# Projections: the short filter of the values on ScalarE and VectorE, sums of squares by GpSimd and small products

## The chip, the cores and the metric

The kernel runs on one of the eight cores of a Trainium2 chip. A core has TensorE (matrix products; the trace gives the clock that was granted to it, as a share of full speed), VectorE, ScalarE and GpSimd (elementwise work, each in its own program order), and a SyncE queue that issues most transfers. In the profile they are PE, DVE, ACT, POOL and SP. Operands lie in SBUF, results of TensorE in PSUM. The metric is the device time of the whole program in microseconds (us). Timelines give the start of an instruction in us from the start of the span.

## The reference

One transformer layer of batch 4, 2048 tokens, width 256, 4 heads of 64: a modulated layer norm, an attention of the delta-rule kind with two causal filters on the values (3 and 31 taps), a router that mixes the branches, an output projection, and a mixture of 16 small experts with a shared one. What matters here are the projections, their four-tap causal filters, and what the later stages take from them (sketched in few lines):

```python
q = silu(causal_dwconv(x @ Wq, conv_q))      # 4 taps per channel
k = silu(causal_dwconv(x @ Wk, conv_k))
v = silu(causal_dwconv(x @ Wv, conv_v))
q = q * rsqrt(sum(q * q, per head) + 1e-6)   # the same for k
fs = fir(v, fir_short)                       # 3 taps per channel
```

The kernel does not scale q and k in this stage. It stores them as they are, and keeps the eight factors per token, `(sum + 1e-6) ** -0.5`, in `rn`, which stays in SBUF.

## The kernel before

The program is a row of stages, each a block that ends when all engines have finished (`EARLY`, `LATE`, `LAST` in `build`): setup, norm_inputs, conv_heads, long_filter, chunk_inverses, delta_scan, mix_and_experts. The change is in conv_heads (L418) and in setup. Tokens come in 16 units of 512 (`NU`, `UT`), a unit in four tiles of 128 (`J`).

A unit has six blocks of 128 channels (`NBLK`), two of k, two of q, two of v. For a block, TensorE multiplies (`project`, into two PSUM buffers `cv_pj`), with the channels on the partitions and the tokens in the free dimension. ScalarE copies the product to `cv_pre` and, scaled by the filter's last tap, to `cv_acc` (`evacuate`, L568). VectorE adds the three other taps, one scalar_tensor_tensor each over 512 tokens, each of which waits for the one before (`conv`, L652). ScalarE applies silu (`silu`, L597) into `cv_kqc` or `cv_vT`; after the sixth block it copies the last columns of `cv_pre` and `cv_vT` to the next unit's buffers (`halo`, `vhalo`).

Later stages want tokens on the partitions. TensorE therefore turns the tiles of k and q (`turn_kq`, into `cv_kqps`) and of v (`turn_v`, into `cv_vfps`). The three-tap filter of the values is made in the second: three products of shifted columns with diagonal matrices `diag_fs` that setup has written. A product of 32-bit operands is two passes in the trace, a transpose is one. ScalarE copies k out (`cv_k`), squares k and q (`cv_sq`), and copies values and filtered values out (`cv_vf`). VectorE sums the squares per head (`reduce_sq`), GpSimd adds the epsilon (L682) and takes the power -1/2 (L686). q is turned for its squares alone: it is stored untouched from `cv_kqc`.

Nothing plans this order; it is written out. `units_ahead` (L240) runs `front(0)` and then `body(u)` for each unit. A body has six slots. In slot s each engine does its share of block s of unit u+1 (`project`, `front_slot`, `conv`) and, in fixed places around it, a tile of unit u's turning. Each engine is strictly in order, so a wait holds up all that is behind it. VectorE's `conv` of block 0 waits for ScalarE's `evacuate` of block 0; ScalarE's `evacuate` of block 0 stands behind `silu`, `halo` and `vhalo` of the unit before, since those are in that unit's slot 5.

## Time and profile before

| | |
|---|---|
| three runs | 2955.58, 2953.98, 2932.95 us (median 2953.98) |
| profiled execution: its time, its span | 2923.57 us, 2921.5 us |
| TensorE's granted clock, mean | 0.896 |
| busy over the span: TensorE, VectorE, ScalarE, GpSimd | 89%, 57%, 38%, 21% |
| conv_heads within the span | first product at 189.5 us, last copy ends at 506.4, next stage's first transfer at 511.7 |
| 288 filter steps of VectorE | 215.7 us busy, 750 ns each |

The busy time of an engine is the time in which an instruction of it is in flight, also where that instruction waits inside the engine. Start to start, two instructions behind one another can be closer than the first one's length. The timeline names for an instruction how long its engine idled before it and what ended that idling. A name that begins with `cv_` belongs to this stage, with `mx_` to the last one.

### The profile page before, as it was taken

What the parts mean: (1) busy time and instruction counts of PE and PEld (TensorE: products, weight loads), DVE (VectorE), ACT (ScalarE), POOL (GpSimd) and SP (SyncE); (2) the same over time, 40 slices, a digit from 0 to 9 for tenths busy, and PEclk for the clock granted to TensorE, in tenths of its full rate; (3) what the DMA queues carried; (4) which work ended last, traced back from release to release, by engine and by line L of the source; (5) the groups of instructions that cost most, each with busy time, mean ns of one, the idle gap of its engine ahead of it and who ended that gap; (6) DMA issues with size and microseconds to landing.
All of it is one profiled execution on the core that took longest, in us unless ns stands there. A gap on an engine that the chain in (4) does not pass through costs nothing.

```text
span 2921.5 us, 40764 instructions
## 1 busy us (share of the span) xinstructions
PE 2613.2 (89%) x14016; PEld 1883.8 (64%) x14016; DVE 1657.9 (57%) x4330; ACT 1108.4 (38%) x2270; POOL 610.6 (21%) x417
## 2 busy tenths in 40 slices
PE   4989998344899799966999999999999999999998
PEld 3966666333688688854666666666656666666665
DVE  3438886220990355535565755675566557665765
ACT  1237787324766222221333233323333333233321
POOL 1105555003110111112122212221222122121210
PEclk7569999675679899986999999999999999999999
DMA  3425555976877677621011101110110111011000
GB/s 92 144 80 173 164 157 162 233 169 139 190 180 187 204 230 240 196 80 44 1 51 51 51 1 52 51 42 10 51 52 16 36 51 51 1 51 51 8 1 15
DMA packets 349603, 274.04 MB, mean 94 GB/s; under 512 B 166413, under 2 KB 306125, under 8 KB 347877
## 3 DMA queue, kind: packets, MB, share of 16 engines
q1 hardware_dynamic: 337680, 256.90, 30.4%
q0 software_dynamic: 3456, 12.58, 1.6%
q10 hardware_dynamic: 8276, 2.10, 0.4%
q8 instruction: 110, 1.80, 0.3%
q14 instruction: 81, 0.66, 0.1%
HBM read 170.65 MB, written 100.89 MB: 93 GB/s over the span
## 4 chain that ended last, share of the span: by engine, by line
PE 37%; DVE 8%; POOL 8%; issue 3%; DMA 0%; POOLq 0%; ACT 0%; DVEq 0%; SPq 0%; ACTq 0%
PE mx_dn L1807 12%; PE mx_up L1793 11%; POOL mx_st L1693 4%; PE mx_m L1746 4%; DVE mx_acc L2098 3%; PE mx_m L1747 2%; PE mx_m L1755 2%; PE mx_m L1770 2%; POOL mx_rms L1704 2%; DVE mx_t L1960 1%; PE mx_m L1784 1%; POOL mx_acc L1711 1%; PE mx_m L1756 1%; POOL mx_acc L1714 1%; DVE mx_t L1962 1%
## 5 line engine op out<-in xcount | busy, mean ns | idle before, releaser
L2098 DVE SCALAR_TENSOR_TENSOR mx_acc<-mx_dn,mx_comb,mx_acc 128x256 f32<-128x256 f32 x1024 | 424.4, 477 | 483.1 <-PE mx_dn L1807 481.0
L1807 PE MATMUL mx_dn<-mx_edn,mx_hs 128*128 128x256 f32 x2048 | 513.2, 396 | 3.3 <-ACT mx_hs L1876 3.3
L1807 PEld LDWEIGHTS mx_dn<-mx_edn,mx_hs 128*128 128x128 f32 x2048 | 398.6, 198 | 168.1 <-issue 95.3
L1793 PE MATMUL mx_up<-mx_h2T,mx_eup 128*128 128x512 f32 x1024 | 500.3, 612 | 0.0
L1876 ACT ACTIVATE mx_hs<-mx_up 128x512 f32<-128x512 f32 x320 | 190.0, 596 | 799.1 <-PE mx_up L1793 798.8
L1793 PEld LDWEIGHTS mx_up<-mx_h2T,mx_eup 128*128 128x128 f32 x1024 | 190.6, 193 | 157.6 <-issue 148.6
L652 DVE SCALAR_TENSOR_TENSOR cv_acc<-cv_pre,conv_w,cv_acc 128x512 f32<-128x512 f32 x288 | 215.7, 750 | 86.9 <-ACT cv_acc L574 80.1
L516 PE MATMUL cv_pj<-cv_hT,wqkv 128*128 128x512 f32 x384 | 181.3, 602 | 14.0 <-ACT cv_acc L574 8.0
L1698 POOL TENSOR_TENSOR mx_t<-mx_vf,mx_ids 128x1024 f32<-128x1024 f32 x16 | 31.5, 1966 | 650.4 <-DVE mx_pr L1955 650.4
L1087 PE MATMUL ci_gps<-ci_kT 64*128 64x128 f32 x768 | 96.9, 412 | 55.4 <-DMA ci_kT<-kqT_d 48.3
L1693 POOL TENSOR_TENSOR mx_st<-mx_tmp,root_pow 128x24 f32<-128x24 f32 x32 | 132.9, 4168 | 31.1 <-DVE mx_tmp L1926 31.1
L806 PE MATMUL fl_ps<-fl_toep,fl_vc 128*84 128x98 f32 x512 | 56.1, 277 | 91.5 <-DMA fl_toep<-taps_d 45.6
L686 POOL TENSOR_TENSOR rn<-cv_ss,half_pow 128x8 f32 x64 | 129.0, 2015 | 11.7 <-POOL cv_ss L682 11.7
L1155 ACT ACTIVATE ci_A<-ci_gps,ck 128x128 f32<-128x128 f32 x384 | 106.0, 373 | 61.2 <-PE ci_gps L1087 61.2
L1807 PEld LDWEIGHTS mx_dn<-mx_sdn,mx_hs 128*128 128x128 f32 x512 | 97.4, 190 | 40.4 <-issue 30.6
L1087 PEld LDWEIGHTS ci_gps<-ci_kT 64*128 64x128 f32 x768 | 79.0, 287 | 68.7 <-DMA ci_kT<-kqT_d 52.0
L1746 PE MATMUL mx_m<-mx_hT,wr 128*128 128x512 f32 x256 | 122.6, 602 | 0.8 <-ACT mx_stT L1836 0.8
L1793 PE MATMUL mx_up<-mx_h2T,mx_sup 128*128 128x512 f32 x256 | 120.0, 602 | 1.4 <-issue 1.4
L1807 PE MATMUL mx_dn<-mx_sdn,mx_hs 128*128 128x256 f32 x512 | 121.0, 379 | 0.0
L516 PEld LDWEIGHTS cv_pj<-cv_hT,wqkv 128*128 128x128 f32 x384 | 67.5, 192 | 74.2 <-issue 54.0
L1488 ACT ACTIVATE ds_U<-ds_ups 64x256 f32<-64x256 f32 x64 | 24.1, 377 | 239.1 <-PE ds_ups L1381 239.1
L806 PEld LDWEIGHTS fl_ps<-fl_toep,fl_vc 128*84 128x84 f32 x512 | 53.5, 178 | 94.1 <-DMA fl_toep<-taps_d 47.2
(229 smaller groups left out, 4399.1 us busy)
## 6 DMA issues: line engine op xcount, KB each, us to landing
kqT_d<-cv_kqc SPq DMA_DIRECT2D x16, 1024.0 KB, 8.0
vf_d<-cv_vf SPq DMA_DIRECT2D x16, 1024.0 KB, 5.3
ds_kqT<-kqT_d SPq DMA_DIRECT2D x16, 1024.0 KB, 5.7
mx_vf<-vf_d SPq DMA_DIRECT2D x16, 1024.0 KB, 6.3
fl_toep<-taps_d SPq DMA_DIRECT2D x32, 392.0 KB, 5.4
ci_kT<-kqT_d POOLq DMA_DIRECT2D x24, 512.0 KB, 5.9
fl_pool<-vf_d SPq DMA_DIRECT2D x8, 1216.0 KB
xin<-_attn_hidden_states_dram SPq DMA_DIRECT2D x16, 512.0 KB, 3.9
```

Of the source, the lines that this page charges most:

```text
L516: ins = pe.matmul(pj[o % 2][:], m.wqkv[:, k, weight(o) * P:(weight(o) + 1) * P], hT[i][:, k, :], start=(k == 0), stop=(k == KD - 1))
L652: ins = dve.scalar_tensor_tensor(out=acc[o % 3][:], in0=pre[i][:, o, t:t + UT], scalar=m.conv_w[:, weight(o), t:t + 1], in1=acc[o % 3][:], ...
L686: pool.tensor_tensor(m.rn[:, bass.ds(u * (J * 2 * H) + j * 2 * H, 2 * H)], ss[j % 2][:], m.half_pow[:, 0:2 * H], ALU.pow).then_inc(rn_done, 1)
L806: ins = pe.matmul(ps[r][0:NA, c // 4, (c % 4) * WIN:(c % 4 + 1) * WIN], vc[:, ch, :], toep[q][:, n * CB + c, ::-1], start=True, stop=True)
L1087: ins = pe.matmul(g_ps[n % 2][h % 2][:, h // 2 * P:(h // 2 + 1) * P], kT[k % 2][r, b, h // 2, :], kT[k % 2][r, b, h // 2, :], start=True, ...
L1155: ins = act.activation(a[:, b, h, :], g_ps[n % 2][h % 2][:, h // 2 * P:(h // 2 + 1) * P], ACT.Identity, scale=m.ck[:, c + h:c + h + 1])
L1693: pool.tensor_tensor(std[:, :, 1, :], tmp[:, 2, part].rearrange("p (a h) -> p a h", h=H), m.root_pow[:, part].rearrange("p (a h) -> p a h" ...
L1746: pe.matmul(out[:], m.wr1[:, k, f * P:(f + 1) * P], hT[i][:, k, :], start=(k == 0), stop=False)
L1793: ins = pe.matmul(up_ps[x % 2][:], lhs, h2T[i][:, k, :], start=(k == 0), stop=(k == KD - 1))
L1807: ins = pe.matmul(dn_ps[(i + n) % 2][:, j, :], hs[x % 4][:, j * P:(j + 1) * P], rhs, start=(x == 0 and j % 2 == 0) or x >= NS, stop=(x >= ...
L1876: act.activation(hs[x % 4][:], up_ps[x % 2][:], ACT.Silu).then_inc(silu_done, 1)
L2098: ins = dve.scalar_tensor_tensor(out=acc[i][:, j, :], in0=dn_ps[(i + n) % 2][:, j, :], scalar=comb[i][:, j, e:e + 1], in1=acc[i][:, j, :], ...
```

## The change

In setup the six diagonal matrices are gone; the filter's weights `fs_w` stay in SBUF as they are loaded.

In conv_heads:
- The value filter is computed with channels on the partitions. ScalarE multiplies `cv_vT` by the last tap into a new tile `cv_ff` (`last_tap`); VectorE adds the two other taps with one scalar_tensor_tensor of 512 tokens each (`fir`), placed between the steps of `conv` in slots 0 and 1. `turn_v` turns both `cv_vT` and `cv_ff` with transposes alone, and moves from slots 1 to 4 to slots 3, 4 and, for two tiles, 5; its evacuation on ScalarE moves with it (`put_vf`).
- Only k is turned (`turn_k`), two tiles into one PSUM bank, with one copy of 512 columns per bank.
- GpSimd squares the four blocks of k and q from `cv_kqc`, and TensorE sums them per head: per tile and block a product with a 128x2 matrix of ones and zeros (`pick`), eight columns a tile, into `cv_ssps`. VectorE adds the epsilon for all four tiles at once, GpSimd takes one power of 32 columns.

The diff, without the declarations of tiles and semaphores:

```diff
--- before.py
+++ after.py
...
@@ -220,12 +219,6 @@
                         .then_inc(vec_step, 1)
             n = 8 + B * KD
 
-            for k in range(KD):
-                for t in range(FIRS):
-                    dve.tensor_scalar(m.diag_fs[:, k, t, :], m.ident[:], fs_w[:, k, t:t + 1], None, ALU.mult)\
-                        .then_inc(vec_step, 1)
-            n += KD * FIRS
-
             dve.wait_ge(act_step, 4)
             for h in range(H):
                 dve.scalar_tensor_tensor(out=m.rtau[:, h:h + 1], in0=taus[:, 4 + h:5 + h], scalar=0.0,
...
@@ -485,7 +485,7 @@
                 sp.wait_ge(silu_done, u * NBLK + (NKQ + 3))
                 sp.dma_start(m.kqT_d[rows].rearrange("j p (a c) -> p a j c", a=NKQ),
                              kqc[i][:].rearrange("p a (j c) -> p a j c", j=J)).then_inc(kqT_store[i], 16)
-                sp.wait_ge(k_done, u * J + (J + 2))
+                sp.wait_ge(k_done, u * 2 + 4)
                 sp.dma_start(m.k_d[rows].rearrange("j p c -> p j c"), k[i][:]).then_inc(store[i], 16)
                 sp.wait_ge(vfe_done, u * J + (J + 2))
                 sp.dma_start(m.vf_d[rows].rearrange("j p c -> p j c"), vf[i][:]).then_inc(store[i], 16)
...
@@ -505,6 +505,7 @@
         @block.tensor
         def _(pe):
             pe.sem_inc(pre_done, 2)
+            pe.wait_ge(pick_done, 3)
 
             def project(u, g, o):
                 i = g % 2
...
@@ -520,28 +521,38 @@
             def turn_v(u, g, j):
                 i = g % 2
                 if j == 0:
-                    pe.wait_ge(silu_done, u * NBLK + (NBLK + 3))
-                    pe.wait_ge(vhalo_done, u + 1)
+                    pe.wait_ge(fir_done, u * KD + KD)
                 pe.wait_ge(vfe_done, u * J + (j + 1))
                 c0 = j * P
                 for k in range(KD):
                     pe.transpose(vf_ps[j % 2][:, k * P:(k + 1) * P],
                                  vT[i][:, k, FIRS - 1 + c0:FIRS - 1 + c0 + P], m.ident[:])
                 for k in range(KD):
-                    for t in range(FIRS):
-                        ins = pe.matmul(vf_ps[j % 2][:, D + k * P:D + (k + 1) * P], vT[i][:, k, c0 + t:c0 + t + P],
-                                        m.diag_fs[:, k, t, :], start=(t == 0), stop=(t == FIRS - 1))
+                    ins = pe.transpose(vf_ps[j % 2][:, D + k * P:D + (k + 1) * P], ff[i][:, k, c0:c0 + P], m.ident[:])
                 ins.then_inc(vf_done, 1)
 
-            def turn_kq(u, g, j):
+            def turn_k(u, g, y):
+                if y == 0:
+                    pe.wait_ge(silu_done, u * NBLK + (NKQ + 3))
+
+                pe.wait_ge(k_done, u * 2 + (y + 1))
+                for j in two:
+                    c0 = (2 * y + j) * P
+                    for k in range(KD):
+                        ins = pe.transpose(k_ps[y][:, j * D + k * P:j * D + (k + 1) * P],
+                                           kqc[g % 2][:, k, c0:c0 + P], m.ident[:])
+                ins.then_inc(kt_done, 1)
+
+            def sum_sq(u, g, j):
+                i = g % 2
                 if j == 0:
-                    pe.wait_ge(silu_done, u * NBLK + (NKQ + 3))
-
-                pe.wait_ge(sq_done, u * J + (j + 1))
-                for a in range(2 * KD):
-                    ins = pe.transpose(kq_ps[j % 2][:, a * P:(a + 1) * P], kqc[g % 2][:, a, j * P:(j + 1) * P],
-                                       m.ident[:])
-                ins.then_inc(kq_done, 1)
+                    pe.wait_ge(sq_done, u * NKQ + NKQ)
+                    pe.wait_ge(eps_done, u + 1)
+                for a in range(NKQ):
+                    ins = pe.matmul(ss_ps[i][:, j * 2 * H + a * 2:j * 2 * H + a * 2 + 2], sq[i][:, a, j * P:(j + 1) * P],
+                                    pick[:], start=True, stop=True)
+                if j == J - 1:
+                    ins.then_inc(ss_done, 1)
 
             def front(u, g):
                 for o in range(NBLK):
...
@@ -551,10 +562,17 @@
                 for s in range(NBLK):
                     if nxt is not None:
                         project(nxt, g + 1, s)
-                    if s < J:
-                        turn_kq(u, g, s)
-                    if 1 <= s < J + 1:
-                        turn_v(u, g, s - 1)
+                    if s < 2:
+                        turn_k(u, g, s)
+                    if s == 1:
+                        sum_sq(u, g, 0)
+                    if s == 2:
+                        for j in range(1, J):
+                            sum_sq(u, g, j)
+                    if s >= 3:
+                        turn_v(u, g, s - 3)
+                    if s == NBLK - 1:
+                        turn_v(u, g, J - 1)
 
             units_ahead(pe, front, body)
 
...
@@ -586,7 +604,7 @@
             def vhalo(u, g):
 
                 if not isinstance(u, int) or u > 0:
-                    act.wait_ge(vf_done, u * J)
+                    act.wait_ge(fir_done, u * KD)
                 if g % UB == UB - 1:
                     src = m.zeros[:, 0:KD * (FIRS - 1)].rearrange("p (a b) -> p a b", a=KD)
                 else:
...
@@ -598,9 +616,16 @@
                 i = g % 2
                 if o == 0:
                     act.wait_ge(kqT_store[i], (u - i) * 8 + 16)
+                    act.wait_ge(ss_done, u + 1)
                 act.wait_ge(conv_done, u * NBLK + (o + 1))
                 dst = kqc[i][:, o, :] if o < NKQ else vT[i][:, o - NKQ, FIRS - 1:]
                 act.activation(dst, acc[o % 3][:], ACT.Silu).then_inc(silu_done, 1)
+
+            def last_tap(u, g, k):
+                i = g % 2
+                act.wait_ge(silu_done, u * NBLK + (NKQ + k + 4))
+                act.activation(ff[i][:, k, :], vT[i][:, k, FIRS - 1:], ACT.Copy, scale=m.fs_w[:, k, FIRS - 1:FIRS])\
+                    .then_inc(tap_done, 1)
 
             def front_slot(u, g, s):
                 evacuate(u, g, s)
...
@@ -610,38 +635,43 @@
                     silu(u, g, s)
                     halo(u, g)
                     vhalo(u, g)
+                    for k in range(KD):
+                        last_tap(u, g, k)
 
             def front(u, g):
                 for s in range(NBLK):
                     front_slot(u, g, s)
 
+            def put_vf(u, i, j):
+                act.wait_ge(vf_done, u * J + (j + 1))
+                act.activation(vf[i][:, j, :], vf_ps[j % 2][:], ACT.Copy).then_inc(vfe_done, 1)
+
             def body(u, g, nxt):
                 i = g % 2
 
                 act.wait_ge(store[i], (u - i) * 16 + 32)
                 for s in range(NBLK):
-                    if s < J:
-                        act.wait_ge(kq_done, u * J + (s + 1))
-                        act.wait_ge(red_done, u * J + (s + 1))
-                        act.activation(k[i][:, s, :], kq_ps[s % 2][:, 0:D], ACT.Copy).then_inc(k_done, 1)
-                        act.activation(sq[s % 2][:], kq_ps[s % 2][:], ACT.Square).then_inc(sq_done, 1)
+                    if s < 2:
+                        act.wait_ge(kt_done, u * 2 + (s + 1))
+                        act.activation(k[i][:, 2 * s:2 * s + 2, :].rearrange("p j c -> p (j c)"), k_ps[s][:], ACT.Copy)\
+                            .then_inc(k_done, 1)
                     if nxt is not None:
                         front_slot(nxt, g + 1, s)
-                    if 1 <= s < J + 1:
-                        act.wait_ge(vf_done, u * J + s)
-                        act.activation(vf[i][:, s - 1, :], vf_ps[(s - 1) % 2][:], ACT.Copy).then_inc(vfe_done, 1)
+                    if s >= 3:
+                        put_vf(u, i, s - 3)
+                    if s == NBLK - 1:
+                        put_vf(u, i, J - 1)
 
             units_ahead(act, front, body)
 
         @block.vector
         def _(dve):
-            dve.sem_inc(red_done, 2)
             dve.sem_inc(rn_done, 2)
             dve.sem_inc(eps_done, 2)
             dve.sem_inc(k_done, 2)
-            dve.sem_inc(sq_done, 2)
-
-            def conv(u, g, o):
+            dve.sem_inc(ss_done, 2)
+
+            def conv(u, g, o, between=None):
                 i = g % 2
                 dve.wait_ge(pre_done, u * NBLK + (o + 3))
                 if o == 0:
...
@@ -653,13 +683,25 @@
                                                    scalar=m.conv_w[:, weight(o), t:t + 1], in1=acc[o % 3][:],
                                                    op0=ALU.mult, op1=ALU.add)
                     ins.then_inc(conv_done if t == CONV - 2 else conv_step, 1)
-
-            def reduce_sq(u, j):
-                dve.wait_ge(sq_done, u * J + (j + 3))
-
-                dve.wait_ge(rn_done, u * J + (j + 1))
-                dve.tensor_reduce(ss[j % 2][:], sq[j % 2][:].rearrange("p (h d) -> p h d", d=DK), AX_X, ALU.add)\
-                    .then_inc(red_done, 1)
+                    if between is not None and t < CONV - 2:
+                        between(t)
+
+            def fir(u, g, k, t):
+                i = g % 2
+                if t == 0:
+                    dve.wait_ge(tap_done, u * KD + (k + 1))
+                    dve.wait_ge(vhalo_done, u + 1)
+                else:
+                    dve.wait_ge(fir_step, u * KD + (k + 1))
+                dve.scalar_tensor_tensor(out=ff[i][:, k, :], in0=vT[i][:, k, t:t + UT], scalar=m.fs_w[:, k, t:t + 1],
+                                         in1=ff[i][:, k, :], op0=ALU.mult, op1=ALU.add)\
+                    .then_inc(fir_done if t == FIRS - 2 else fir_step, 1)
+
+            def add_eps(u, g):
+                i = g % 2
+                dve.wait_ge(ss_done, u + 3)
+                dve.wait_ge(rn_done, u + 1)
+                dve.tensor_scalar(ss[i][:], ss_ps[i][:, 0:J * 2 * H], L2_EPS, None, ALU.add).then_inc(eps_done, 1)
 
             def front(u, g):
                 for o in range(NBLK):
...
@@ -667,27 +709,42 @@
 
             def body(u, g, nxt):
                 for s in range(NBLK):
-                    if 1 <= s < J + 1:
-                        reduce_sq(u, s - 1)
+                    taps = None
+                    if s < KD:
+                        taps = lambda t: fir(u, g, t, s)
                     if nxt is not None:
-                        conv(nxt, g + 1, s)
+                        conv(nxt, g + 1, s, taps)
+                    elif taps is not None:
+                        for k in range(KD):
+                            taps(k)
+                    if s == NBLK - 2:
+                        add_eps(u, g)
 
             units_ahead(dve, front, body)
 
         @block.gpsimd
         def _(pool):
-            def body(u):
-                for j in range(J):
-                    pool.wait_ge(red_done, u * J + (j + 3))
-                    pool.tensor_tensor(ss[j % 2][:], ss[j % 2][:], m.l2_eps[:, 0:2 * H], ALU.add)\
-                        .then_inc(eps_done, 1)
-
-                    pool.wait_ge(eps_done, u * J + (j + 3))
-                    pool.tensor_tensor(m.rn[:, bass.ds(u * (J * 2 * H) + j * 2 * H, 2 * H)], ss[j % 2][:],
-                                       m.half_pow[:, 0:2 * H], ALU.pow).then_inc(rn_done, 1)
-
-            with pool.Fori(0, NU) as u:
-                body(u)
+            pool.memset(pick[:], 0.0).then_inc(pick_done, 1)
+            pool.wait_ge(pick_done, 1)
+            for hh in two:
+                pool.memset(pick[hh * DK:(hh + 1) * DK, hh:hh + 1], 1.0).then_inc(pick_done, 1)
+
+            def front(u, g):
+                i = g % 2
+                pool.wait_ge(ss_done, u + 1)
+                for a in range(NKQ):
+                    pool.wait_ge(silu_done, u * NBLK + (a + 4))
+                    pool.tensor_tensor(sq[i][:, a, :], kqc[i][:, a, :], kqc[i][:, a, :], ALU.mult).then_inc(sq_done, 1)
+
+            def body(u, g, nxt):
+                i = g % 2
+                if nxt is not None:
+                    front(nxt, g + 1)
+                pool.wait_ge(eps_done, u + 3)
+                pool.tensor_tensor(m.rn[:, bass.ds(u * (J * 2 * H), J * 2 * H)], ss[i][:], m.half_pow[:, 0:J * 2 * H],
+                                   ALU.pow).then_inc(rn_done, 1)
+
+            units_ahead(pool, front, body)
 
 
 def long_filter(nc, m, w):
...
```

Two places show how the instructions stand. The first is VectorE in the loop over units; a row is an instruction with its line, what it writes and reads, and its size (ISA and REGISTER_ALU rows compute counts to wait for). Before, the end of slot 1 and slot 2:

```order
L652 SCALAR_TENSOR_TENSOR cv_acc<-cv_pre,conv_w,cv_acc 128x512
L658 REGISTER_ALU
L660 REGISTER_ALU
L661 TENSOR_REDUCE cv_ss<-cv_sq 128x8
L646 REGISTER_ALU
L652 SCALAR_TENSOR_TENSOR cv_acc<-cv_pre,conv_w,cv_acc 128x512
```

Each of slots 1 to 4 had a reduction ahead of its block's three steps. Now, VectorE in slot 0:

```order
L678 REGISTER_ALU
L682 SCALAR_TENSOR_TENSOR cv_acc<-cv_pre,conv_w,cv_acc 128x512
L692 ISA
L696 SCALAR_TENSOR_TENSOR cv_ff<-cv_vT,fs_w,cv_ff 128x512
L681 ISA
L682 SCALAR_TENSOR_TENSOR cv_acc<-cv_pre,conv_w,cv_acc 128x512
L692 REGISTER_ALU
L696 SCALAR_TENSOR_TENSOR cv_ff<-cv_vT,fs_w,cv_ff 128x512
L681 REGISTER_ALU
L682 SCALAR_TENSOR_TENSOR cv_acc<-cv_pre,conv_w,cv_acc 128x512
```

Two steps of the value filter stand between the three of block 0, behind its first one. The same holds in slot 1, and slots 2 to 5 have their block's three steps, slot 4 also the addition of the epsilon.

The second place is ScalarE between two units, from the halo of the one to the scaled copy of the next one's block 0. Before:

```order
L584 ACTIVATE cv_pre<-cv_pre 128x6x3
L589 REGISTER_ALU
L593 REGISTER_ALU
L595 ACTIVATE cv_vT<-cv_vT 128x2x2
L624 REGISTER_ALU
L626 ACTIVATE cv_k<-cv_kqps 128x256
L627 ACTIVATE cv_sq<-cv_kqps 128x512
L570 ISA
L571 ACTIVATE cv_pre<-cv_pj 128x512
L573 REGISTER_ALU
L574 ACTIVATE cv_acc<-cv_pj,conv_w 128x512
```

Now, from the second halo copy on:

```order
L613 ACTIVATE cv_vT<-cv_vT 128x2x2
L627 ACTIVATE cv_ff<-cv_vT,fs_w 128x512 x2
L646 REGISTER_ALU
L647 ACTIVATE cv_vf<-cv_vfps 128x512
L646 REGISTER_ALU
L647 ACTIVATE cv_vf<-cv_vfps 128x512
L655 REGISTER_ALU
L656 ACTIVATE cv_k<-cv_kps 128x512
L588 ISA
L589 ACTIVATE cv_pre<-cv_pj 128x512
L591 REGISTER_ALU
L592 ACTIVATE cv_acc<-cv_pj,conv_w 128x512
```

Between the halo copies and the two copies of block 0 there were two instructions, and there are five.

## Rows read from the trace of the kernel before

**Rows 1.** Window of one unit: PE, PE loads, DVE, ACT, POOL busy, clock.
```profile
299.99:319.08 19.09, 18.76 (x98) 12.37 (x97) 15.55 (x24) 15.32 (x33) 10.62 (x9) 1.00 0.53 165
```

**Rows 2.** Waits from 200 to 500 us: total us, times, longest us.
```profile
DVE cv_acc L652 <- ACT cv_acc L574: 48.7, 31, 3.4
```

**Rows 3.** Timeline between two units: start, length, engine, line; bracket: idle before.
```profile
302.53 2.33 DVE L652 SCALAR_TENSOR_TENSOR cv_acc<-cv_pre,conv_w,cv_acc 128x512 f32<-128x512 f32 x3 [0.22 <-ACT cv_acc L574]
...
304.89 0.63 ACT L603 ACTIVATE cv_vT<-cv_acc 128x512 f32<-128x512 f32 x1 [1.87 <-DVE cv_acc L652]
...
305.69 0.38 ACT L626 ACTIVATE cv_k<-cv_kqps 128x256 f32<-128x256 f32 x1
...
305.97 0.59 ACT L627 ACTIVATE cv_sq<-cv_kqps 128x512 f32<-128x512 f32 x1
...
306.45 0.60 ACT L571 ACTIVATE cv_pre<-cv_pj 128x512 f32<-128x512 f32 x1
...
306.92 0.70 ACT L574 ACTIVATE cv_acc<-cv_pj,conv_w 128x512 f32<-128x512 f32 x1
...
307.75 2.33 DVE L652 SCALAR_TENSOR_TENSOR cv_acc<-cv_pre,conv_w,cv_acc 128x512 f32<-128x512 f32 x3 [2.89 <-ACT cv_acc L574]
...
309.99 0.68 DVE L661 TENSOR_REDUCE cv_ss<-cv_sq 128x8 f32<-128x512 f32 x1
...
310.59 2.32 DVE L652 SCALAR_TENSOR_TENSOR cv_acc<-cv_pre,conv_w,cv_acc 128x512 f32<-128x512 f32 x3
```

**Rows 4.** Single lines: ns least/median/greatest; last row: busy us, mean ns.
```profile
L652 DVE SCALAR_TENSOR_TENSOR cv_acc<-cv_pre,conv_w,cv_acc x288: 739/752/753, 194.3 to 495.5; 128x512 f32<-128x512 f32 x144
...
L682 POOL TENSOR_TENSOR cv_ss<-cv_ss,l_eps x64: 199/638/642, 214.9 to 504.6; 128x8 f32<-128x8 f32 x64
...
L225 DVE TENSOR_SCALAR diag_fs<-ident,fs_w 128x128 f32<-128x128 f32 x6 | 1.3, 278 | 0.0
```

**Rows 5.** Timeline of the last stage, VectorE and GpSimd (POOL) together.
```profile
1329.58 1.23 DVE L1960 TENSOR_TENSOR mx_t<-mx_fl,mx_pr 128x1024 f32<-128x1024 f32 x1
...
1329.63 2.94 POOL L1698 TENSOR_TENSOR mx_t<-mx_vf,mx_ids 128x1024 f32<-128x1024 f32 x1 [25.62 <-DVE mx_pr L1955]
...
1330.73 2.92 DVE L1962 TENSOR_TENSOR mx_t<-mx_dl,mx_pr 128x1024 f32<-128x1024 f32 x1
...
1333.68 2.83 DVE L1966 TENSOR_TENSOR mx_t<-mx_t 128x1024 f32<-128x1024 f32 x1
...
1423.22 1.90 POOL L1698 TENSOR_TENSOR mx_t<-mx_vf,mx_ids 128x1024 f32<-128x1024 f32 x1 [50.96 <-DVE mx_pr L1955]
...
1423.99 1.66 DVE L2098 SCALAR_TENSOR_TENSOR mx_acc<-mx_dn,mx_comb,mx_acc 128x256 f32<-128x256 f32 x4 [0.85 <-PE mx_dn L1807]
```

**Rows 6.** Groups of instructions, GpSimd (POOL): busy us, mean ns.
```profile
L1714 POOL TENSOR_TENSOR mx_acc<-mx_acc,mx_x 128x1024 f32<-128x1024 f32 x16 | 37.5, 2345 | 1.3
...
L1693 POOL TENSOR_TENSOR mx_st<-mx_tmp,root_pow 128x24 f32<-128x24 f32 x32 | 132.9, 4168 | 31.1 <-DVE mx_tmp L1926 31.1
```

**Rows 7.** Groups of instructions, TensorE (PE): busy us, mean ns.
```profile
L516 PE MATMUL cv_pj<-cv_hT,wqkv 128*128 128x512 f32 x384 | 181.3, 602 | 14.0 <-ACT cv_acc L574 8.0 <-DMA cv_hT<-hT_d 6.0
...
L1784 PE MATMUL mx_m<-wgT,mx_h2T 128*128 128x16 f32 x256 | 31.4, 265 | 0.9 <-ACT mx_h2T L1864 0.9
```

**Rows 8.** Timeline of the stage's end; last row: a window, as in rows 1.
```profile
496.31 0.63 ACT L603 ACTIVATE cv_vT<-cv_acc 128x512 f32<-128x512 f32 x1 [1.87 <-DVE cv_acc L652]
...
496.99 0.69 PE L528 MATMUL cv_vfps<-ident,cv_vT 128*128 128x128 f32 x2 [3.41 <-ACT cv_vT L603]
...
497.48 2.69 PE L532 MATMUL cv_vfps<-diag_fs,cv_vT 128*128 128x128 f32 x12
...
500.66 1.50 PE L532 MATMUL cv_vfps<-diag_fs,cv_vT 128*128 128x128 f32 x12
...
505.76 0.60 ACT L632 ACTIVATE cv_vf<-cv_vfps 128x512 f32<-128x512 f32 x1 [0.96 <-PE cv_vfps L532]
...
497.00:500.00 3.00, 3.00 (x14) 3.00 (x15) 1.37 (x2) 1.66 (x6) 1.12 (x2) 0.51 0.90 249
```

22 lines of the change are left out of this document (14 added, 8 removed).

## The prediction

> **What bounds the kernel now.** I first read the table of time windows. The projection stage runs from about 189 to 512 us. Its engines repeat one pattern per unit of 512 tokens, and a unit takes 19.1 us; within one, TensorE is busy 18.8 us, VectorE 15.6, ScalarE 15.3, GpSimd 10.6 [rows 1]. By busy share TensorE is the limit. The table of waits says something else: it shows 31 times that VectorE's short filter waited for ScalarE's scaled copy, 48.7 us in all [rows 2]. The timeline shows where. Once per unit, after the filter of block 5, VectorE stands 2.89 us, and ScalarE is busy without a gap all through it: the last silu (304.89), the two small halo copies, then the k copy (305.69), the square (305.97), the unscaled copy of the next unit's block 0 (306.45) and the scaled one (306.92), which lets VectorE start at 307.75 [rows 3]. Everything else in the unit is VectorE work back to back: three filter steps of 2.24 us start to start, and four reductions of 0.60 us [rows 3]. So two engines set the pace in turn: 16.2 us of VectorE plus 2.9 us in which ScalarE walks its list make the 19.1 us, and TensorE just fits beside it. What counts is the work on VectorE, and what stands on ScalarE's list between block 5's silu and the next block 0.
>
> **The change on VectorE.** It removes four reductions per unit: 4 x 0.60 = 2.4 us. It adds four steps of the value filter, of the form of the projection filter's steps, which take 739 to 753 ns [rows 4]; an instruction that waits for no result of its predecessor starts some 0.08 us before that one's end (the reduction at 309.99 against an end at 310.08 [rows 3]), so 0.67 to 0.75, taken 0.70: 2.8 us. The sums of squares now come from PSUM in one instruction of 32 columns, at most a few tenths; I take 0.2 us, between nothing and the 0.68 of a reduction [rows 3]. Net: +0.6 us. The six diagonal matrices of setup go (278 ns each [rows 4]): at most 1.3 us gained once.
>
> **The squares on GpSimd** are the part that looks free, since that engine is idle almost half of the unit. I think it is not. Two places of the last stage have elementwise GpSimd and VectorE instructions together. At 1329.58 VectorE multiplies two SBUF operands in 1.23 us; GpSimd's multiplication, issued at 1329.63, takes 2.94 instead of its usual 1.90 (that of 1423.22); VectorE's next one at 1330.73 takes 2.92 instead of 1.2, and the one after it 2.83, beside a second product of GpSimd [rows 5]. They take turns. Beside it, VectorE's four instructions at 1423.99 that read one operand from PSUM take 1.66 us together while GpSimd multiplies [rows 5], 0.41 each: no delay. The projection filter reads both `cv_pre` and `cv_acc` from SBUF, so it is of the first kind. The filter shows GpSimd's side already: the tiny addition of L682 has a median of 638 ns and a minimum of 199, while none of the 288 filter steps is over 753 ns [rows 4]; so today's eight-column GpSimd reads cost VectorE nothing, and a 512-column one will. A product of 1024 contiguous columns takes 2.345 us [rows 6], so one of 512 about 1.17, and with the faster form of 1.90, 0.95. VectorE was lengthened by 1.69 (2.92 less 1.23) and 1.60 us (2.83 less 1.23) per GpSimd instruction of 1.90, thus by 0.26 less than its length. That makes 0.91 us for a square; bounds 0.69 (0.95 less 0.26) and the full 1.17. All four squares come right after a silu, when VectorE filters the next block, so none lands in its idle time: 4 x 0.91 = 3.6 us a unit. The Trainium skill, "SBUF — State Buffer", section "SBUF: two separate sides", gives the rule: the port pair is an exclusive lock for a whole instruction, and it names VectorE instructions with two SBUF inputs as taking it against a GpSimd instruction that reads SBUF. Applied literally the whole 1.17 us of a square would count, 17 us more over the 64 squares than in my sum; the trace agrees with the turns but shows 0.26 us less each. The power of 32 columns, about 5.2 us by the 4.168 of 24 columns [rows 6], takes GpSimd's idle time during block 5 and the gap; its few reads I cost at nothing, as those of the eight-column ones. GpSimd's sum is then about 10 us of work per unit, and nobody waits for it: TensorE asks for the squares one block after the last one is made.
>
> **ScalarE's list between the units.** Gone from it are the half-width k copy (0.28 from start to start) and the square (0.48). New are two last-tap multiplications, put in right after the halo copies, one full-width k copy, and two `cv_vf` evacuations that stood at slots 3 and 4 and now stand behind slot 5. Start to start: silu and halos 0.80 (304.89 to 305.69); taps, between the 0.48 of a plain and the 0.70 of a whole scaled copy, taken 0.57 each, 1.14; two evacuations and the k copy at 0.48, 1.44; unscaled copy 0.47; scaled copy until VectorE starts 0.83 (306.92 to 307.75) [rows 3]. Sum 4.7 us against 2.9. VectorE can't use the gap: its value-filter steps stand behind the first step of block 0, which waits. So **+1.8 us a unit**. In the other slots ScalarE loses 0.75 us each and waits; nothing there shortens the path.
>
> **TensorE** loses twelve passes with diagonal matrices per tile, keeps six transposes (two of k and four of v where four and two stood), and gains eight passes of two columns. By the rows, per unit: 24 passes at 0.47 us (181.3 / 384) [rows 7], 24 transposes at about 0.11 (the price of a pass in the twelve of 1.50 us at 500.66 [rows 8]), 32 small passes at 0.123 (31.4 / 256, for 16 columns [rows 7]): 17.9 us. The same prices give 19.7 for today's 18.8, so the change is worth 1.8 us and leaves 17.0. I cost it at nothing: VectorE and ScalarE hide it with 7 to 8 us to spare.
>
> **The sum.** Per unit 16.2 - 2.4 + 2.8 + 0.2 + 3.6 + 4.7 = 25.1 us against 19.1. Fifteen rounds of VectorE slots at +4.2 make 63.0; fourteen gaps at +1.8 make 25.2; the first unit has its squares, 3.6, and a gap without `cv_vf`, +0.9. The last unit's tail now takes 10.05 us from the last silu (496.31) to the end of the last evacuation (505.76 + 0.60) [rows 8]; afterwards two taps, four filter steps and four lighter tiles, about 7.5: -2.5, with GpSimd's last power just inside the final store. Setup -1.3. Together 63.0 + 25.2 + 4.5 - 2.5 - 1.3 = **+88.9 us**. The profiled execution took 2923.57 us, so 3012; the median of the three runs shown is 30.4 higher, and I predict against that: 2953.98 + 88.9 = 3043 us.
>
> **Rivals.**
> (a) GpSimd's squares do not hold VectorE up in this stage. For it: every filter step today keeps to 753 ns beside a busy GpSimd [rows 4]. Against: those GpSimd reads are of eight columns, and the turns of [rows 5]. Then 54.0 + 3.6 us go away: +31, 2985 us, just at the 1% line.
> (b) TensorE's clock. Its work gets lighter, and between the small products and block 2 of the next unit (which waits for the end of the gap) it idles some 3 to 4 us. After 3.41 us idle, twelve passes took 2.69 us at 497.48 where they take 1.50 at 500.66, and in that stretch the granted clock fell to its lower level of 1.2 GHz (0.51 over 497 to 500 us [rows 8]). If that happens in each unit, project blocks and small products of the first slots double; with two blocks of lead, the fourth block comes 1 to 2 us late: +15 to +30, so about 3066 us. The Trainium skill, "TensorE: Matmul & The Clock Gate", section "HAM oscillation — how this bites in real kernels", describes such a loop, where each round's wait makes the next burst start slow.
> (c) Faster: the unit is really bound by TensorE, and VectorE's gap is only its slack. For it: 18.8 of 19.1 us busy [rows 1]. Then the unit falls by what TensorE loses, 1.8 us, 16 times: -29, and 2925 us. VectorE has 16.8 us of work even with no square in its way, so any gain needs a gap below 2.3 us, and this one a gap of 0.5; silu, halos and the two copies alone are 2.1. Against it stands that ScalarE shows no wait in the gap [rows 3].
> (d) The scheme does not run as written, for example a stall on the semaphores of the sums: place unknown, either side.
>
> **Numbers.** Forecast 0.62, (a) 0.12, (b) 0.18, (c) 0.05, (d) 0.03. The range goes from (a), 2980, to (b) with the upper price of the squares, 3043 + 30 + 17 = 3090. About 1% is what can be told from no change. (c) is faster; (a) lies on the line of 1%, so most of it counts as same: faster 0.06, same 0.10, slower 0.84.
>
> **What would show it.** Right: units 24 to 26 us apart; some filter steps of 1.5 us or more, about four a unit, each beside a GpSimd square; squares that last up to 1.9 us; one VectorE wait of 4.5 to 5 us a unit on ScalarE's scaled copy. Wrong: filter steps all at 750 ns (then (a)); a granted clock under 0.9 in the stage and waits of ScalarE for `cv_pj` (then (b)); units under 19 us (then (c)). A gap that shows ScalarE waiting for TensorE or GpSimd would break the second term.

## The result, and the profile after

The changed kernel takes 2988.93 us (median of 4 runs, 2981.21 to 3001.03) against 2949.30 us of the kernel before beside it (4 runs): ratio 1.0171, 95% interval 1.0115 to 1.0227. It is slower, by more than the noise and by less than 2.3%. The ratios here and below are those on record for executions in the chip's faster state, a second and slower one being left out, and need not equal the ratio of the medians, which is 1.013 here (39.6 us). The forecast was 3043 us, range 2980 to 3090, so the time lies near the lower end of the range. The profiled execution took 2990.27 us (span 2988.5), 66.7 more than the profiled one of before.

By stages, from the first load of one to the first load of the next, the difference has one place:

| us | ahead | projections | long filter | chunk inverse | delta | last stage | span |
|---|---|---|---|---|---|---|---|
| before | 185.3 | 326.4 | 173.0 | 284.4 | 317.6 | 1634.9 | 2921.5 |
| after | 184.4 | **403.6** | 173.7 | 284.1 | 317.8 | 1624.9 | 2988.5 |

The projection stage is 77.2 us longer; the last one is 10 us shorter, by a scatter that it also shows between copies of one kernel (below).

The page of the changed kernel, first its totals (busy time, share of the span, instructions), then three of its costliest groups:

```profile
PE 2633.6 (88%) x13760; PEld 1876.9 (63%) x13760; DVE 1708.7 (57%) x4340; ACT 1098.7 (37%) x2206; POOL 607.6 (20%) x372
...
L682 DVE SCALAR_TENSOR_TENSOR cv_acc<-cv_pre,conv_w,cv_acc 128x512 f32<-128x512 f32 x288 | 263.3, 932 | 111.8 <-ACT cv_acc L592 107.1
...
L517 PE MATMUL cv_pj<-cv_hT,wqkv 128*128 128x512 f32 x384 | 230.0, 732 | 56.1 <-ACT cv_acc L592 50.9
...
L737 POOL TENSOR_TENSOR cv_sq<-cv_kqc 128x512 f32<-128x512 f32 x64 | 72.7, 1135 | 208.8 <-ACT cv_kqc L622 208.8
```

The same 288 filter steps took 215.7 us before (750 ns each) and take 263.3 now. The single lines say how (ns least/median/greatest): most steps are as before, some are twice as long, and the squares have their own long ones.

```profile
L682 DVE SCALAR_TENSOR_TENSOR cv_acc<-cv_pre,conv_w,cv_acc x288: 734/751/1634, 192.7 to 571.2; 128x512 f32<-128x512 f32 x144
...
L696 DVE SCALAR_TENSOR_TENSOR cv_ff<-cv_vT,fs_w,cv_ff x64: 737/744/750, 214.1 to 575.5; 128x512 f32<-128x512 f32 x64
...
L737 POOL TENSOR_TENSOR cv_sq<-cv_kqc x64: 1038/1040/1602, 197.2 to 567.3; 128x512 f32<-128x512 f32 x64
```

The steps of the projection filter kept to 753 ns in [rows 4]. Here is one square with the step beside it, and ahead of them the gap between two units, from the timeline of the changed kernel (start, length, engine, line; in brackets the idle time before, and what ended it):

```profile
309.65 0.63 ACT L622 ACTIVATE cv_vT<-cv_acc 128x512 f32<-128x512 f32 x1 [1.70 <-DVE cv_acc L682]
...
310.42 1.32 ACT L627 ACTIVATE cv_ff<-cv_vT,fs_w 128x512 f32<-128x512 f32 x2
311.65 1.06 ACT L647 ACTIVATE cv_vf<-cv_vfps 128x512 f32<-128x512 f32 x2
312.60 0.59 ACT L656 ACTIVATE cv_k<-cv_kps 128x512 f32<-128x512 f32 x1
...
313.08 0.60 ACT L589 ACTIVATE cv_pre<-cv_pj 128x512 f32<-128x512 f32 x1
313.55 0.70 ACT L592 ACTIVATE cv_acc<-cv_pj,conv_w 128x512 f32<-128x512 f32 x1
...
314.31 3.58 PE L517 MATMUL cv_pj<-cv_hT,wqkv 128*128 128x512 f32 x4 [2.94 <-ACT cv_acc L592]
314.38 0.75 DVE L682 SCALAR_TENSOR_TENSOR cv_acc<-cv_pre,conv_w,cv_acc 128x512 f32<-128x512 f32 x1 [4.76 <-ACT cv_acc L592]
...
315.05 0.75 DVE L696 SCALAR_TENSOR_TENSOR cv_ff<-cv_vT,fs_w,cv_ff 128x512 f32<-128x512 f32 x1
...
315.71 0.75 DVE L682 SCALAR_TENSOR_TENSOR cv_acc<-cv_pre,conv_w,cv_acc 128x512 f32<-128x512 f32 x1
...
318.36 0.74 DVE L696 SCALAR_TENSOR_TENSOR cv_ff<-cv_vT,fs_w,cv_ff 128x512 f32<-128x512 f32 x1
...
318.58 1.42 POOL L737 TENSOR_TENSOR cv_sq<-cv_kqc 128x512 f32<-128x512 f32 x1 [5.25 <-ACT cv_kqc L622]
...
319.02 1.53 DVE L682 SCALAR_TENSOR_TENSOR cv_acc<-cv_pre,conv_w,cv_acc 128x512 f32<-128x512 f32 x1
```

VectorE stands 4.76 us where it stood 2.89 [rows 3], and ScalarE works without a break all through it. Right behind, TensorE's four passes take 3.58 us, while such a block takes 1.88 at full clock (a row of the second experiment shows it). The five steps of slot 0 start 0.66 us apart (314.38, 315.05, 315.71), since each stands next to one that it does not depend on. At the square, the step that already runs when it starts (318.36) keeps its 0.74 us and the square waits for it (1.42 us instead of 1.04); the next step, at 319.02, then waits for the square and takes 1.53. The waits of VectorE from 200 to 580 us (total, times, longest), which were 48.7 us in 31 over 200 to 500 us in [rows 2]:

```profile
DVE cv_acc L682 <- ACT cv_acc L592: 75.2, 17, 4.8
```

And a window of the stage, with the columns of [rows 1]:

```profile
250.00:450.00 200.00, 170.51 (x670) 100.71 (x669) 157.13 (x191) 123.53 (x234) 84.35 (x42) 0.86 0.40 126
```

The unit [rows 1] was 19.1 us long with the clock at 1.00; from the load of 239.07 to that of 504.37 there are now eleven units, 24.1 us each, and the granted clock is 0.86 over this window.

### The profile page after: what moved, and what is told of

Its sections match the earlier page's. It is cut to its first block, busy times and chain, and to the rows that moved or that the text cites. A ratio compares the mean times of both kernels' runs of the same rounds, so it can differ in the third digit from the quotient of the medians.

```text
span 2988.5 us, 40061 instructions
## 1 busy us (share of the span) xinstructions
PE 2633.6 (88%) x13760; PEld 1876.9 (63%) x13760; DVE 1708.7 (57%) x4340; ACT 1098.7 (37%) x2206; POOL 607.6 (20%) x372
## 4 chain that ended last, share of the span: by engine, by line
PE 37%; DVE 8%; POOL 7%; issue 2%; DMA 0%; ACT 0%; POOLq 0%; DVEq 0%; SPq 0%; ACTq 0%
PE mx_dn L1864 12%; PE mx_up L1850 11%; POOL mx_st L1750 4%; PE mx_m L1803 4%; DVE mx_acc L2155 3%; PE mx_m L1812 2%; PE mx_m L1804 2%; PE mx_m L1827 2%; POOL mx_rms L1761 2%; DVE mx_t L2017 1%; PE mx_m L1841 1%; POOL mx_acc L1768 1%; PE mx_m L1813 1%; POOL mx_acc L1771 1%; DVE mx_t L2019 1%
## 5 line engine op out<-in xcount | busy, mean ns | idle before, releaser
L682 DVE SCALAR_TENSOR_TENSOR cv_acc<-cv_pre,conv_w,cv_acc 128x512 f32<-128x512 f32 x288 | 263.3, 932 | 111.8 <-ACT cv_acc L592 107.1
L517 PE MATMUL cv_pj<-cv_hT,wqkv 128*128 128x512 f32 x384 | 230.0, 732 | 56.1 <-ACT cv_acc L592 50.9
L517 PEld LDWEIGHTS cv_pj<-cv_hT,wqkv 128*128 128x128 f32 x384 | 79.2, 228 | 121.6 <-issue 66.0
L1750 POOL TENSOR_TENSOR mx_st<-mx_tmp,root_pow 128x24 f32<-128x24 f32 x32 | 132.9, 4168 | 28.1 <-DVE mx_tmp L1983 28.1
L737 POOL TENSOR_TENSOR cv_sq<-cv_kqc 128x512 f32<-128x512 f32 x64 | 72.7, 1135 | 208.8 <-ACT cv_kqc L622 208.8
L1545 ACT ACTIVATE ds_U<-ds_ups 64x256 f32<-64x256 f32 x64 | 24.1, 377 | 239.4 <-PE ds_ups L1438 239.4
```

The lines of the kernel that those rows point to most:

```text
L517: ins = pe.matmul(pj[o % 2][:], m.wqkv[:, k, weight(o) * P:(weight(o) + 1) * P], hT[i][:, k, :], start=(k == 0), stop=(k == KD - 1))
L682: ins = dve.scalar_tensor_tensor(out=acc[o % 3][:], in0=pre[i][:, o, t:t + UT], scalar=m.conv_w[:, weight(o), t:t + 1], in1=acc[o % 3][:], ...
L737: pool.tensor_tensor(sq[i][:, a, :], kqc[i][:, a, :], kqc[i][:, a, :], ALU.mult).then_inc(sq_done, 1)
L1750: pool.tensor_tensor(std[:, :, 1, :], tmp[:, 2, part].rearrange("p (a h) -> p a h", h=H), m.root_pow[:, part].rearrange("p (a h) -> p a h" ...
```

## The experiments

Two theories each explain half of the loss: the squares on GpSimd make VectorE's filter steps longer, and ScalarE's longer list between two units makes VectorE wait. The expectations call the two together theory A. The rival (b) of the prediction, the clock of TensorE, is their theory B. Theory D, in the last two of these runs, is that both hold: once the squares are gone, the low clock takes their place. In each diff the change is against the changed kernel, if nothing else is said; "stage" is the projection stage of the profiled execution.

**The changed kernel again**, as a base for the others. The kernel is the same, without an edit.

> The changed kernel as it is, on the chip and in the call of the next three. Theory A (VectorE's program is lengthened by two things: GpSimd's squares that take turns with it at 0.74 us each, and a gap of 4.75 us between units in which ScalarE walks its list): units 24 us apart, stage of 403 to 404 us, whole kernel 1.5 to 2.3% over the kernel before. Theory B (TensorE's lowered clock after the gap makes the units longer) expects the same here.

Measured: stage 404.1 us against 403.6, as expected; ratio 1.0195 (1.0142 to 1.0248). So the stage repeats to half a us, and single numbers of it can be compared between runs; the whole time scatters more.

**Squares over 8 columns instead of 512.** All the instructions stay; the rest of `cv_sq` is filled with ones once, at the start, so the computation of the sums is left out in the main.

```diff
+  for i in two:
+      pool.memset(sq[i][:], 1.0).then_inc(pick_done, 1)
...
-  pool.tensor_tensor(sq[i][:, a, :], kqc[i][:, a, :], kqc[i][:, a, :], ALU.mult)
+  pool.tensor_tensor(sq[i][:, a, 0:8], kqc[i][:, a, 0:8], kqc[i][:, a, 0:8], ALU.mult)
```

> GpSimd squares only the first 8 of each 512 columns (64 instructions as before, the rest of the tile is the constant 1), so the sums of squares are left out in the main. Everything else is the changed kernel. Theory A: the filter steps all go back to 735 to 755 ns; a unit loses 4 x 0.74 = 3.0 us (24.1 to 21.1), 64 squares give about 47 us less than the control, and the gap of 4.75 us stays. Theory B: what lengthens the unit is TensorE's clock after the gap, which stays too, so less than 15 us are gained, and ScalarE's waits for cv_pj take up the rest.

Measured: the filter steps fall back to what they were before,

```profile
L682 DVE SCALAR_TENSOR_TENSOR cv_acc<-cv_pre,conv_w,cv_acc x288: 741/751/792, 191.5 to 545.2; 128x512 f32<-128x512 f32 x144
```

so it is the width of the squares that lengthens them. Their busy time is 213.2 us here, 50.1 less than in the changed kernel: 0.78 us for each of 64 squares. (The 0.74 and 47 us of the expectations come from the 215.7 us of the kernel before, whose steps are not interleaved.) But the stage is 378.7 us and not 357, ratio 1.0137 (1.0086 to 1.0188): of 50 us of VectorE time only 25 came back. Something else had stood behind it. The timeline of this kernel shows what, in one of its longer units:

```profile
276.17 5.12 PE L552 MATMUL cv_ssps<-cv_pick,cv_sq 128*128 128x2 f32 x24
...
281.14 3.76 PE L517 MATMUL cv_pj<-cv_hT,wqkv 128*128 128x512 f32 x4
...
284.94 0.60 ACT L589 ACTIVATE cv_pre<-cv_pj 128x512 f32<-128x512 f32 x1 [3.75 <-PE cv_pj L517]
...
285.46 1.88 PE L517 MATMUL cv_pj<-cv_hT,wqkv 128*128 128x512 f32 x4
...
286.15 3.98 DVE L682 SCALAR_TENSOR_TENSOR cv_acc<-cv_pre,conv_w,cv_acc 128x512 f32<-128x512 f32 x5 [3.35 <-ACT cv_acc L592]
```

TensorE works through the small products and the next block at half speed, the block is late, ScalarE waits 3.75 us for it and VectorE 3.35 for ScalarE; from 285.46 a block takes 1.88 again. Units of 20.5 to 22.3 us come between units of 23.9 to 24.5. This is rival (b), which had been invisible as long as the squares kept VectorE late anyway.

**The gap filled.** ScalarE's last tap of the first tile is brought forward, ahead of block 5's silu, the last tap of the second comes right behind `halo`, the copies for the next block 0 come next, and the evacuations of `cv_vf` and k behind those; VectorE does the four steps of the value filter ahead of block 0, so that it works on them during ScalarE's list. So the order changes on both engines.

```diff
-  evacuate(u, g, s)                       # first of every slot
   if s >= 1:
+      evacuate(u, g, s)
       silu(u, g, s - 1)
   if s == NBLK - 1:
+      last_tap(u, g, 0)
       silu(u, g, s)
       halo(u, g)
+      last_tap(u, g, 1)
+      evacuate(u + 1, g + 1, 0)           # if there is a next unit
       vhalo(u, g)
-      for k in range(KD):
-          last_tap(u, g, k)
...
   def body(u, g, nxt):                    # VectorE
+      for k in range(KD):
+          for t in range(FIRS - 1):
+              fir(u, g, k, t)             # no longer between the steps of blocks 0 and 1
```

> Only the order changes: ScalarE makes the first last-tap product before the last silu, then silu, halo, second last-tap, and at once the two copies of the next unit's block 0; the two late cv_vf evacuations and the k copy follow behind. VectorE does its four value-filter steps first in a unit, while ScalarE works on that list. Squares stay on GpSimd. Theory A: VectorE's gap shrinks from 4.75 us to under 0.6, the work stays 19.3 us, so units of 19.3 to 20.0 us, 15 x 4.3 = 60 us less than the control, near the kernel before (within 1%). Theory B: as the gap goes, the clock stays at full speed and the gain is the same or larger; if instead TensorE's work bounds the unit (17.0 us) nothing of this differs. A rival C (ScalarE's total list is the bound, about 16 us of work per unit and in order) expects the gap to reappear as small waits: units of 21 us or more.

Measured: stage 349.2 us, 54 less where 60 were expected; ratio 1.0043 (0.9992 to 1.0095). Units are 20.3 us apart, a little over the 19.3 to 20.0 expected. From the timeline:

```profile
314.10 0.72 ACT L627 ACTIVATE cv_ff<-cv_vT,fs_w 128x512 f32<-128x512 f32 x1
315.65 3.08 DVE L699 SCALAR_TENSOR_TENSOR cv_ff<-cv_vT,fs_w,cv_ff 128x512 f32<-128x512 f32 x4
...
317.53 0.68 ACT L592 ACTIVATE cv_acc<-cv_pj,conv_w 128x512 f32<-128x512 f32 x1
...
318.64 1.53 DVE L685 SCALAR_TENSOR_TENSOR cv_acc<-cv_pre,conv_w,cv_acc 128x512 f32<-128x512 f32 x2
```

Four value-filter steps stand where the gap was, and the next block 0 follows them with no idle time. VectorE is busy 191.1 of the 200 us from 250 to 450, against 157.1: now it is the bound, with the squares still lengthening its steps (least/median/greatest 741/752/1633 ns), and the granted clock in that window is 0.97.

**The kernel before with a product on GpSimd added**: one of 512 columns behind each of its powers, nobody reads it. This adds the one suspected cost to the other kernel; the diff is against the kernel before.

```diff
   pool.tensor_tensor(..., m.half_pow[:, 0:2 * H], ALU.pow).then_inc(rn_done, 1)
+  pool.tensor_tensor(extra[j % 2][:], src[:], src[:], ALU.mult).then_inc(extra_done, 1)
```

> The kernel before with four extra GpSimd products of 128x512 by itself per unit, from a constant tile into a scratch tile, one behind each power. Nobody uses them. Theory A: each holds VectorE's two-SBUF-operand filter steps up by 0.7 to 0.9 us when it meets one; filter steps of up to 1.7 us appear; 64 products cost 35 to 50 us against the kernel before. Theory B and any theory in which GpSimd works beside VectorE for free: no change (within 0.3%), filter steps stay at 753 ns at most.

Measured, by the page's group:

```profile
L655 DVE SCALAR_TENSOR_TENSOR cv_acc<-cv_pre,conv_w,cv_acc 128x512 f32<-128x512 f32 x288 | 243.8, 852 | 84.5 <-ACT cv_acc L577 77.7
```

The filter steps take 28.1 us more than before, 0.44 per product, and the stage 24.6 us more (351.0). The mechanism works in the old kernel too. The size is below the 35 to 50 us expected, and the longest step is 1.41 us. The timeline from 300 to 315 us shows why: three products of a unit each lengthen a block's steps by about 0.65 us (2.98 instead of 2.33 for three steps), and the fourth (312.20, 1.03 us) falls into VectorE's gap and costs nothing. That makes 31 us over 16 units. The time of the whole, ratio 1.0052 (0.9975 to 1.0129), can't be told from no change, so this run is evidence by its trace alone.

**The evacuations of `cv_vf` and k behind the next block 0**: only ScalarE's order is changed, the copies for the next block 0 move ahead of them.

```diff
-  evacuate(u, g, s)                       # first of every slot
   if s >= 1:
+      evacuate(u, g, s)
...
       for k in range(KD):
           last_tap(u, g, k)
+      evacuate(u + 1, g + 1, 0)           # if there is a next unit
```

> The changed kernel with one move: ScalarE's two copies of the next unit's block 0 stand ahead of the two late cv_vf evacuations and the k copy instead of behind them. Theory A: the gap loses three list entries of 0.48 us, 4.75 to about 3.3 us, and the units 1.45 us each, some 21 us in all against the changed kernel. If the moved copies then delay the second slot, the gain is smaller (10 us). Theory B: TensorE's idle time shrinks from 3.1 to under 2 us, its clock no longer falls, so more than 30 us.

Measured: the gap is 3.3 us instead of 4.8,

```profile
DVE cv_acc L685 <- ACT cv_acc L592: 60.9, 22, 3.3
```

and the stage 389.4, 14.7 less instead of 21. The ratio, 1.0143 (1.0074 to 1.0212), can't be told from that of the changed kernel. Fourteen gaps of 1.45 us are 20. Most units are 22.1 to 22.7 us apart, but some take 23.6 to 24.6, and there it goes as in the second experiment: in the unit from 375.63, TensorE needs 5.12 us for the 24 small products and 3.53 for the next block, and VectorE then waits 2.02 us for ScalarE at 386.63. Theory B is out with its number, and in part with its reason: TensorE's idle time is down to 1.5 to 1.7 us, as it expected, but the clock still falls (0.88 from 250 to 450 us, 0.86 before the move).

**The squares on ScalarE**, one per slot 2 to 5, and none on GpSimd.

```diff
+  def square(u, g, a):
+      act.wait_ge(silu_done, u * NBLK + (a + 4))
+      act.activation(sq[g % 2][:, a, :], kqc[g % 2][:, a, :], ACT.Square).then_inc(sq_done, 1)
...
       silu(u, g, s - 1)
+  if 2 <= s < NKQ + 2:
+      square(u, g, s - 2)
...
-  pool.tensor_tensor(sq[i][:, a, :], kqc[i][:, a, :], kqc[i][:, a, :], ALU.mult).then_inc(sq_done, 1)
```

> The changed kernel with the four squares per unit made by ScalarE (one 128x512 activation each, behind the silu of the next block) instead of GpSimd. Theory A: the filter steps go back to 735 to 755 ns, 3.0 us less per unit; ScalarE gets 2.1 us more work, of which slots 3 and 4 (silu, square, two copies, one evacuation: 2.6 us beside 2.24 us of VectorE) show about 0.4 us each: units of 21.5 to 22 us, 33 to 40 us less than the changed kernel. If GpSimd's products cost nothing, this is slower than the changed kernel by up to 10 us.

Measured: steps of 739/752/840 ns, so nothing holds VectorE up, and yet a stage of 399.3, only 4.8 less; ratio 1.0154 (1.0094 to 1.0214). The expectation was missed by some 30 us. VectorE's waits for ScalarE are 118.2 us from 200 to 560 us, and ScalarE's for TensorE:

```profile
ACT cv_pre L589 <- PE cv_pj L517: 39.7, 16, 4.4
```

Units of about 22.5 and 25.1 us alternate for most of the stage. The removed cost was replaced nearly in full. That it was the chain of the second experiment is shown further down, where TensorE is kept busy.

**Both: the gap filled and the squares on ScalarE.** The edits are those two together.

> The order of e3 together with the squares on ScalarE, as in e6. Theory A: VectorE has 16.6 us of work per unit and nothing in its way, ScalarE 16.1, TensorE 17.0; units of 17.3 to 18.2 us against 19.1 before and 24.1 in the changed kernel; stage some 15 to 28 us shorter than in the kernel before, 0.5 to 1% faster than it. Rival: ScalarE's full list binds, units of 19 us or more and no gain over the kernel before.

Measured: stage 315.9 us, 88 less than the changed kernel and 10.5 less than before, where 15 to 28 were expected; median 2908.19 us (12 runs), ratio 0.9920 (0.9875 to 0.9965). It is the only version below the kernel before. From 250 to 450 us:

```profile
250.00:450.00 200.00, 191.41 (x873) 118.62 (x874) 179.33 (x252) 178.22 (x351) 59.71 (x11) 0.97 0.55 172
```

Three engines are busy nine tenths of it, units are 18.3 us apart, and VectorE's single waits are 0.45 us on average (22.7 us in 50). The scheme of the change is worth something once neither of its two costs is there.

**TensorE kept busy between the units**, with four products of 448 columns that nobody reads, issued ahead of where it would wait. Nothing else is changed.

```diff
   if s == 1:
       sum_sq(u, g, 0)
+      for r in range(4):
+          pe.matmul(ss_ps[g % 2][:, 64:512], m.ident[:], m.wqkv[:, 0, 0:448], start=True, stop=True)
```

> The changed kernel with four products of 448 columns per unit that nobody uses, put where TensorE idles about 3 us in the gap (behind the first small products of sums, into unused columns of the same bank). They fill the idle time. Theory A: the granted clock of the stage goes up to 0.97 to 1.00, TensorE's waits vanish, and the time stays as in the changed kernel within 0.3%, since no wait of VectorE ended with TensorE. Theory B: with the full clock, blocks 2 and 3 come earlier and the stage is 15 to 30 us shorter.

Measured: the clock over 250 to 450 us rises from 0.86 to 0.97, and the stage is 399.8, 3.8 less; ratio 1.0193 (1.0139 to 1.0246). ScalarE's waits for `cv_pj` fall from 21.1 us to 2.7. So in the changed kernel as it stands the low clock costs at most 4 us.

**The same four products with the 8-column squares, and with the squares on ScalarE.** If the clock is what took the gain away in those two, it must come back here, though TensorE has more to do.

> e2 (GpSimd squares 8 of 512 columns, so the sums of squares are left out in the main) together with the four unused products of e8 that fill TensorE's idle time in the gap. e2 took 378.7 us for the stage where A expected 357, and half of its units showed 24 small products in 5.1 us and a project block in 3.8, behind which VectorE waited 3.4. Theory D (both hold: squares cost 0.74 us each, and as soon as they are gone TensorE's lowered clock takes their place): the clock of the stage rises to 0.97 or more, all units take 20.5 to 21.3 us, stage 353 to 360 us. Theory A' (the missing part of e2 has another cause, such as ScalarE's list): stage as in e2, 375 to 382 us.

> e6 (squares on ScalarE) together with the same four unused products of TensorE in the gap. e6 took 399.3 us for the stage. Theory D: the clock stays up, VectorE's waits on late project blocks vanish, units of 21.5 to 22.2 us, stage 362 to 372 us. Theory A': ScalarE's fuller list is what bound e6, stage within 5 us of 399.

Measured: stages of 348.7 us (378.7 without the products; 4 below the expected range) and 362.3 (399.3 without; at its lower end). The clock over 250 to 450 us is 0.99 and 0.96, against 0.83 in both without the products. Ratios 1.0034 (0.9996 to 1.0071) and 1.0102 (1.0059 to 1.0145). One unit by the window, of the kernel with 8-column squares:

```profile
272.92:297.31 24.39, 21.88 (x80) 14.06 (x80) 15.69 (x23) 14.90 (x30) 6.99 (x5) 0.79 0.41 130
```

With TensorE kept busy:

```profile
274.11:294.96 20.85, 20.06 (x90) 12.12 (x89) 15.62 (x23) 14.82 (x30) 6.94 (x5) 1.00 0.48 151
```

The first is long because TensorE is slow, not because it has much to do: the second has ten more of its instructions and takes 3.5 us less. The timeline of the second at the place of the four rows above:

```profile
277.38 2.74 PE L552 MATMUL cv_ssps<-cv_pick,cv_sq 128*128 128x2 f32 x24
...
279.97 1.96 PE L517 MATMUL cv_pj<-cv_hT,wqkv 128*128 128x512 f32 x4
...
280.97 7.60 DVE L684 SCALAR_TENSOR_TENSOR cv_acc<-cv_pre,conv_w,cv_acc 128x512 f32<-128x512 f32 x10
```

24 small products take 2.74 us instead of 5.12, the block 1.96 instead of 3.76, and VectorE has ten steps in a row. The stages side by side (us):

| | squares on GpSimd | of 8 columns | on ScalarE |
|---|---|---|---|
| otherwise as changed | 403.6 | 378.7 | 399.3 |
| TensorE kept busy | 399.8 | 348.7 | 362.3 |
| gap filled | 349.2 | not run | 315.9 |

Alone, the squares are worth 25 us, the clock 4; together they are worth 55. Each removed by itself is replaced by the other. The two kernels with TensorE kept busy also give the price of a square with nothing to hide it: 399.8 less 348.7 is 51.1 us, 0.80 for each of 64. The squares on ScalarE give back 37.5 of these 51; the rest I have not taken apart.

**The kernel before, twice more**, since its unprofiled runs and its profiled one disagreed.

> The kernel before, unchanged, one look more. So far its one profile has 326.4 us in the stage and 2595.1 in all the rest, while its unprofiled runs have a median of 2936 to 2949 us; the changed kernel's profiles agree with its runs. If the stage itself scatters in the kernel before, its length here differs from 326 by more than 5 us. If the scatter lies in the later stages, the stage stays within 1 us of 326.4 and the rest differs by 10 to 20 us.

> The same once more, for the same question: stage within 1 us of 326.4, the rest somewhere between 2577 and 2615 us.

Measured: 2942.83 and 2942.91 us against the first profile's 2923.57. Their projection stages are 326.6 and 326.3, as before; the chunk inverse is 308.5 and 304.9 where it was 284.4. Windows from its middle and its end, of the first profile of before:

```profile
800.00:850.00 50.00, 46.03 (x319) 40.24 (x318) 47.19 (x85) 23.26 (x77) 6.18 (x4) 0.59 0.73 181
...
900.00:950.00 50.00, 48.41 (x553) 43.19 (x550) 0.00 (x0) 28.87 (x90) 0.00 (x0) 1.00 0.71 177
950.00:968.00 18.00, 14.50 (x168) 12.89 (x168) 0.00 (x0) 9.39 (x29) 0.00 (x0) 0.89 0.56 154
```

And of the first repeat:

```profile
800.00:850.00 50.00, 45.01 (x301) 39.19 (x302) 47.19 (x87) 20.78 (x68) 6.25 (x4) 0.56 0.72 173
...
900.00:950.00 50.00, 48.21 (x457) 43.04 (x456) 0.00 (x0) 23.85 (x75) 0.00 (x0) 0.82 0.68 170
950.00:990.00 40.00, 39.69 (x272) 35.62 (x272) 0.00 (x0) 14.96 (x47) 0.00 (x0) 0.50 0.25 61
```

In both, the granted clock is at its lower level, 1.2 GHz, for some 40 us in the middle of the stage (0.50 from 804 to 844 us in the first profile), although TensorE has no idle time there. The first repeat has a second such stretch at the end, where TensorE is busy nearly all the time. The second repeat has none at its end (0.97 from 950 to 990 us) but a longer one in the middle: 0.50 from 834 to 904 us, TensorE busy throughout. The stage takes 24 and 20 us more. So the base has more than one value, and the first profile was one with the least of these falls.

## Why the prediction was right, and where its sizes were off

**The bound.** It said that VectorE's work and ScalarE's list between the units set the pace in turn, with TensorE hidden. This holds: the gap filled takes 54 us off the stage, the squares moved or shortened take 37 to 51 (with the clock held), while TensorE's lighter work gave nothing. The 54 us are not the list alone, since the clock is back at 0.97 with the gap gone. The 1.8 us by which TensorE's work was to fall do not follow from the rows: 48 passes at 0.11 less 32 at 0.123 are 1.3. It was costed at nothing, so this touches only rival (c).

**The gap, +1.8 us a unit.** Predicted 4.7 us, measured 4.76, from the start-to-start times of [rows 3]. The third experiment shows it to be the order and not the amount of work: the same operations in another order on ScalarE and VectorE leave no gap. ScalarE's order alone took 1.45 us off it.

**The squares, 3.6 us a unit.** The mechanism was right, the size too large. The turns of [rows 5] were carried over to a place where the trace of before had no such pair; measured are 0.80 us for a square, not 0.91, which is 3.2 a unit and 7 us less over the 64. The length was mis-sized, the deduction was not: a square alone took 1.04 us and not the 1.17 taken from the longer product of [rows 6], and less the 0.26 of [rows 5] this makes 0.78. Both bounds of the text are excluded, the full length of a square and 0.69. The full length was the rule of the Trainium skill, "SBUF — State Buffer", section "SBUF: two separate sides", the port pair as a lock for a whole instruction; the trace agrees with who meets whom, since all these steps read two SBUF operands and the one issued during a square is the one that lasts until after it (319.02), but per square VectorE loses 0.24 us less than the square's 1.04.

**The value filter, 2.8 us a unit.** This term was mis-sized too. A step that stands behind an independent one starts 0.66 us after it (314.38, 315.05, 315.71), not 0.70. And the interleaving shortens the projection filter as well: alone, its dependent steps start 0.79 us apart (three in 2.33 us at 0.75 each, [rows 3]). Five interleaved steps take 3.3 us from start to start where three took 2.24, so a slot grows by 1.07 and the unit by 2.1. The addition of the epsilon takes 0.1 from start to start (331.14 to 331.24), not 0.2. With this the unit's sum is 16.2 - 2.4 + 2.1 + 0.1 + 3.2 + 4.76 = 24.0 us; measured 24.1, predicted 25.1. One us for each of fifteen units is 15 us less than forecast, and the tail, next, took 3 of them back: 12 of the 13 by which the stage's forecast of +90.2 was above the +77.2 measured.

**The tail, -2.5.** From the last silu (572.02) to the end of the last evacuation (580.10 + 0.60) it is 8.7 us against 10.05: -1.4; and the next stage begins 7.3 us after that instead of 5.3. The last wait was costed as unchanged, and it took the gain: +0.6 in all. GpSimd's last power now ends 1.2 us behind the last evacuation (581.85), where it ended 0.3 behind (506.66); whether that or the final store lengthens the wait is not shown.

**Rival (a)**, squares that cost nothing, is out by the steps of 1.6 us. Its number was the nearest of all, though: 2985 us, 4 off the measured 2988.93, where the forecast is 54 off. By the time alone one would have picked the wrong mechanism. The nearness comes from the base (below): against the profiled executions (a) gives 2955 us, 35 below the 2990.27 measured, and the forecast's 3012 is 22 above. **Rival (c)**, TensorE as the bound, is out as well: units are 24.1 us apart and not under 19. **Rival (b)**, the clock, was taken as an alternative with a price of its own, +15 to +30 on top. This was the weak step: its signs are all there (clock 0.86, ScalarE waiting 21.1 us for `cv_pj`), and its price is about 4 us (3.8 and 4.3 against the two traces of the changed kernel), because the squares keep VectorE behind TensorE's half-speed blocks. It is a second limit beneath the first. The prediction's list of signs could not tell the two apart: it took a clock under 0.9 and waits for `cv_pj` to mean (b). The Trainium skill, "TensorE: Matmul & The Clock Gate", section "HAM oscillation — how this bites in real kernels", describes the loop of a wait and a slow next burst; the trace agrees where nothing covers it (3.75 us of ScalarE's wait behind blocks of 3.76 us instead of 1.88 to 1.96), and the forecast by that rule, 3066 us, is 77 us above the time measured.

**The base.** The sum was made against the profiled execution (3012, measured 2990.27: 13 us from the stage, 10 from a last stage that ran 1624.9 instead of 1634.9). To reach the median I added the 30.4 us by which the runs lay above that profile. That was the largest error, and a choice: the changed kernel's runs (2981 to 3001) lie around its profile. Two more traces of before, 19 us longer than the first, show where such a difference can lie: the chunk inverse, a stage that the change leaves alone, takes 24 and 20 us more, with a longer part of it at half speed. Of the ten traces of the changed kernel and its variants one has a chunk inverse that is longer in this way (the last run with TensorE kept busy, 298.7 us; the others 280 to 286), of the four of before and its variant two. With such an execution as the base, 2990.27 less 2942.83 is 47 us, beside the 50 that the ratio gives (34 to 67). A lower clock in some executions is not peculiar to the kernel before. Those of the experiments have their mean clock on record, and the time follows it: the kernel before took 2909 to 2933 us at 0.893 to 0.902 and 2936 to 2958 at 0.884 to 0.891, beside the kernel with both costs removed, which took 2894 to 2913 at 0.889 to 0.895 in seven executions and 2929 to 2941 at 0.878 to 0.883 in five. In which stage the unprofiled ones lost the clock is not shown, nor why it falls in one and not in the next. The last stage, 1617 to 1638 us over all fourteen traces, scatters by about 20 us in kernels that are the same there, and the delta stage took 327.2 us in one trace (TensorE kept busy) where the others have 317 to 318; neither is taken apart here.

## What to carry to other kernels

An engine that is half idle isn't free: ask what its new instruction and the busy engine's read at the same time, and price the turns per instruction, from the nearest pair in the trace. When the limit of a stage is a list of small operations on one engine, write down its order and who waits for which entry; here a new order was worth 54 us, more than either removed cost alone. And where removing one suspected cost brings less than its busy time says, take the next limit away with it before the theory is given up: here two removals of 25 and 4 us made 55 together. And read the executions' granted clock before one profile is taken as the base.

## What the runs showed of the hardware

- The granted clock of TensorE fell in units in which it had idled 1.5 to 4.1 us in one piece, and half speed held on for the work behind it: 24 products of two columns took 5.12 us instead of 2.74, four of 512 columns 3.58 to 3.76 instead of 1.88 to 1.96. With the gap filled, where it idled about 1.0 us, it was 0.97 over 250 to 450 us; with four unused products in the gap, 0.96 to 0.99.
- It was also at half speed in the chunk inverse while TensorE was busy without a break: some 40 us in the middle of the stage in the first profile of before, a second stretch at the end in the first repeat (39.7 of 40 us busy at 0.50), and 70 us or more in the second. The rows read here don't tell these executions from one another before it falls.
- A power of 32 columns on GpSimd took 5.43 to 5.87 us beside 4.17 for 24 columns in [rows 6], while a product of 512 columns took 1.04 us.
- Two GpSimd and VectorE instructions that meet both get longer: a product from 1.04 to as much as 1.60 us, VectorE's step from 0.75 to as much as 1.63. With nothing to hide it, VectorE lost 0.80 us per product. Products of eight columns cost it nothing that shows (no step over 0.79 us).
- VectorE's steps of 512 columns, 0.75 us long, started 0.66 us apart when independent and 0.79 when each needed the one before.
